# A fused recurrence and gated block on one core: 60 gate units in 56 slots instead of 60, and 25 instead of 24 output products in a slot

## The chip, the cores and the metric

The kernel runs on one core of one Trainium2 chip. The metric is the device time of one execution in microseconds (us). All engines of the core take part: PE (TensorE, the matmuls), DVE (VectorE), ACT (ScalarE), POOL (GpSimd) and SP (SyncE, which here issues every DMA of the stage that is described below).

## What is computed

The input is a sequence of 2048 tokens with 1024 features. After a layernorm two branches run, and the result is `x + s * silu(ffn)`:

```python
xn = _layernorm(x)
# recurrent branch
proj = xn @ W_in.T;  x, gate = proj[..., :2048], proj[..., 2048:]
x = silu(causal_conv4(x));  ts, B, C = rms(split(x @ W_x.T));  dt = softplus(ts @ W_dt.T + b_dt)
state = state * exp(dt * A) + (dt * x) * B          # per token, 2048 channels x 16 states
y = (state . C + x * D) * silu(gate);  s = y @ W_out.T
# gated block with 4-bit weights and low-rank parts
g = _qlinear(xn, gate_q, ...);  u = _qlinear(xn, up_q, ...);  f = _qlinear(silu(g) * u, down_q, ...)
out = x + s * silu(f)
```

A product of 32-bit numbers is made of 16-bit ones: each operand is split into a high and a low part, and three products (high with high, high with low, low with high) are added up in PSUM.

## The kernel before

**Two parts.** A first part (lines 180 to 1000) normalizes and transposes x, forms the convolved branch, dt, B and C, and stores what the second part reads. The second part is a loop over 256 **slots** that every engine goes through in its own queue. A slot is one state index n of one step; a step (16 slots) is 512 tokens of 512 channels. All engines hold the loop over slots as straight code and meet by semaphores alone.

**The scan, in every slot.** POOL multiplies the injection (L1660, one operation of 128x2048) some three slots ahead, in a ring of four. ACT forms four decays (L1384). DVE runs four scans (L1524), and between them it adds three transposed blocks of the slot before into the sum over states (`add_up`, L1542, and L1536 where n is 0); ACT and POOL handle the fourth block (L1422, L1672). PE transposes the slot before in four groups of four (`turn`, L1710). Before the first group of a slot PE waits for the four scans of the slot before; DVE's first `add_up` of a slot waits for that first group. In slots with n = 3, 7, 11, 15, from step 1 on, PE transposes one block back (`y_back`, L1721) and DVE makes one more operation (`d_u`, L1551).

**The other work, as filler of PE between the groups of transposes** (the function `piece` and its neighbours), by slot number s:

- s = 0 to 59, the **gate units**: unit u = s + 4 (u = 0 to 3 are made before the loop) is a tile of 128 gate channels for 512 tokens, 24 products, in four pieces of six (`gate_product`, L1733). In slot s + 1 ACT takes the tanh (L1442), DVE multiplies (L1576) into `gout[u % 2]`, and SP stores that to `gs_s` (L1250). DVE's multiplication of unit u waits until the store of unit u - 2 has landed, since both use one of two buffers. The weights come in halves of 128x512 f32: SP loads half h to `gr` (L1150), ACT scales and rounds it (L1403, L1406), POOL forms the low part (L1638).
- s = 60 to 147, the 88 FFN units, two products of eight double parts each (L1752, L1754, L1763).
- s = 150 to 213, the down product, four slots to each of 16 token tiles (L1780).
- s = 216 to 255, the **output product** with W_out: 1536 products in 32 results of 48, of which 24 are made in a slot (`out_product`, L1828). A result is added up by DVE (L1558) and POOL and stored by SP. The first 36 products read a quarter of W_out's converted halves, which SP loads after the last down product (L1339).
- After slot 255, the rest of the output products: 4 times (12 products and a `y_back`), then up to result 24, then a wait for the last step's y (`e_y`, loads; `e_lo`, four small operations of DVE and ACT that follow the last `y_back`, L1628), then the results 24 to 31.

**SP's queue.** SP goes through the same slots as a list of waits and DMA issues, in this order within a slot: W_out piece; in odd slots the broadcast load of B (`load_bb`, L1146), which waits for the injection of slot s + 2 to be done; the load of a gate half; the store of the gate unit made on PE in slot s - 2; conversions of the down weights (L1254, L1258); loads and stores of the FFN; where n is 2 the four loads of the next step (L1302, L1305, 512 KB each); y stores; down and output transfers. What waits in this list holds everything behind it.

**Order of the phases.** `FF0` is the slot in which the FFN begins, and `DOWN0`, `OUT0` follow from it; `DQ_AT` and `WO_AT` are the slots of the two weight conversions. The lines that set the amounts:

```python
FF0 = GATES - EARLY                       # 64 - 4 = 60
if s < FF0: gate_product(s + EARLY, 2 * u, 2 * u + 2)          # piece u of a slot, eighths of a unit
def out_cut(s): return 24 * (s - OUT0), 24 * (s - OUT0 + 1)
first = 24 * (SLOTS - OUT0)               # output products made before the loop ends
```

Of the kernel before, what the change touches and what calls it, by code (L numbers as in the profile page):

```python
# [33 lines left out]
T = 512  # L34
# [3 lines left out]
HK = H // P  # L38
DT = DI // P
J = 4  # L40
G = DT // J
IT = -(-I // P)
# [5 lines left out]
LEAD = 1  # L48
# [4 lines left out]
    "s_const s_gsc s_dec s_dub s_inj s_scan s_carry s_turn s_sum s_ev s_acc s_yt s_yev s_gate s_yhi s_parts s_ug0 s_ug1 "  # L53
    "s_ys0 s_ys1 s_u15 s_bb0 s_bb1 s_bb2 s_bb3 s_dt0 s_dt1 s_du0 s_du1 s_wq0 s_wq1 s_bt0 s_bt1 s_conv s_g s_u s_scg "
    "s_scu s_lg s_lu s_ex s_sg s_h s_hi s_lo s_hs0 s_hs1 z_in z_sc z_hi z_lo z_mm z_ex z_g z_st0 z_st1 c_in q_cv c_st "
# [5 lines left out]
SLOTS = STEPS * N  # L61
GATES = DT * C
EARLY = C
FF0 = GATES - EARLY
# [13 lines left out]
DQ_AT = tuple(7 * i // 3 for i in range(IT))  # L78
# [3 lines left out]
def mixer_kernel(nc, x, win, convw, convb, wx, wdt, bdt, alog, dskip, wout, gu_q, g_scale, u_scale,  # L82
# [3 lines left out]
    with whole:  # L86
# [85 lines left out]
        s_dec, s_inj = sem("s_dec"), sem("s_inj")  # L172
        z_in, z_sc, z_hi, z_lo, z_mm, z_ex, z_g = (sem("z_" + a) for a in "in sc hi lo mm ex g".split())
        inj = sb(whole, "inj", [P, RING, J, T])
        with ExitStack() as st:
# [52 lines left out]
            (f_const, f_nv, f_sd, f_xn, f_tp, f_xh, f_xl, f_sc, f_hi, f_lo, f_z, f_mm, f_cv, f_e, f_u, f_wx,  # L228
             f_hl, f_hs, f_sm, f_rv, f_rq, f_rm, f_tt, f_ts, f_tl, f_bt, f_pre, f_mx, f_nab, f_ex, f_ln, f_dt, f_a, f_b, f_ap,
             f_bl, f_bs, f_du, f_ru, f_dv) = (sem("f_" + a) for a in (  # L230
                "const nv sd xn tp xh xl sc hi lo z mm cv e u wx hl hs sm rv rq rm tt ts tl bt pre mx nab ex ln dt a b ap "
# [46 lines left out]
            with nc.Block() as block:  # L278
                @block.sync
                def _(sp):  # L280
# [78 lines left out]
                    for u in range(LAST + 2):  # L359
# [10 lines left out]
                        if u == LAST:  # L370
                            sp.wait_ge(f_mm, LEAD + LAST - 1)
                            for half in range(2):
                                sp.dma_start(gout[:, half, :], win[DT, :, half * T:(half + 1) * T]).then_inc(z_in, 16)
# [43 lines left out]
                    sp.dma_start(gr[:, :], win[DT + 1, :, 0:T]).then_inc(z_in, 16)  # L417
                    store_bt(C - 1)
                    sp.wait_ge(f_rm, LEAD + 4 * C)
                    sp.dma_start(gr_next[:, :], win[DT + 1, :, T:2 * T]).then_inc(z_in, 16)  # L420
# [16 lines left out]
                def _(act):  # L437
# [67 lines left out]
                    def gate_high(half, src):  # L505
                        act.activation(src, src, ACT.Copy, scale=WS).then_inc(z_sc, 1)
# [60 lines left out]
                    act.wait_ge(z_in, LEAD + 32)  # L567
# [21 lines left out]
                    act.wait_ge(z_in, LEAD + 64)  # L589
# [414 lines left out]
        with ExitStack() as st:  # L1004
# [48 lines left out]
            (s_const, s_gsc, s_dub, s_scan, s_carry, s_turn, s_sum, s_ev, s_acc, s_yt, s_yev, s_gate, s_yhi, s_parts,  # L1053
             s_u15, s_conv, s_g, s_u, s_scg, s_scu, s_lg, s_lu, s_ex, s_sg, s_h, s_hi, s_lo) = (sem("s_" + a) for a in (
                "const gsc dub scan carry turn sum ev acc yt yev gate yhi parts u15 conv g u scg scu lg lu ex sg h hi lo"
# [46 lines left out]

            def out_cut(s):

                return 24 * (s - OUT0), 24 * (s - OUT0 + 1)
# [33 lines left out]
            with nc.Block() as block:  # L1139
                @block.sync  # L1140
                def _(sp):
# [7 lines left out]
                    def load_gate(half, dst):  # L1149
                        sp.dma_start(dst, win[DT + half // 2, :, half % 2 * T:(half % 2 + 1) * T]).then_inc(z_in, 16)  # L1150
# [75 lines left out]
                    for m, src in enumerate((g_scale, u_scale)):  # L1226
                        sp.dma_start(gsc[:, m, :], src).then_inc(s_const, 16)
                    for s in range(SLOTS):
# [147 lines left out]
                def _(act):  # L1376
# [23 lines left out]
                    def gate_high(half, src):  # L1400
                        w, r = divmod(half, 2)
                        act.wait_ge(z_in, LEAD + max(16 * half + 16, 32))
# [26 lines left out]
                    act.wait_ge(s_const, LEAD + 32)  # L1429
# [4 lines left out]
                    for s in range(SLOTS):  # L1434
# [3 lines left out]
                        u = s - 1 + EARLY  # L1438
                        if EARLY - 1 <= u < GATES:
# [26 lines left out]
                        half = (s + EARLY + 3) // 2  # L1466
                        if s % 2 == 1 and half < 2 * DT:
                            gate_high(half, gr[:, :])
# [498 lines left out]
```

## Time and profile before

| what | us |
|---|---|
| median of 3 runs (lowest, highest) | 2778.59 (2778.08, 2783.23) |
| the profiled execution | 2781.2 |
| its span, first to last instruction | 2779.4 |
| gate units from slot 3 to the end of slot 59 | 424.45 |
| FFN, slots 60 to 147 | 815.75 |
| down product and its surroundings, slots 148 to 215 | 538.38 |
| output product, slots 216 to 255 | 289.20 |
| after the last slot | 133.67 |

The slot limits are read from the timeline of DVE: a slot begins with the first of its four scans. The page says that PE is busy for 97% of the span, DVE for 86%, POOL for 71% and ACT for 57%, with a mean granted TensorE clock of 0.993. The busy time of PE counts the modelled end of each matmul, so neighbours overlap in it; distances between starts tell what a piece takes. In a timeline row the first number is the start, the second the length, and a bracket names the idle time before it and what ended it. In a row of a stretch the numbers are the length, then the busy time of each engine with its instructions, the granted clock, the DMA engines' busy share and the rate in GB/s. A row of DMA issues ends with the size and the median time from issue to landing.

### The profile page before, as it was taken

Reading aid. Unit: us, or ns where it says so; the run is one execution under the profiler, and the core shown is the slowest. Engines: PE = TensorE matmul, PEld = TensorE weight load, DVE = VectorE, ACT = ScalarE, POOL = GpSimd, SP = SyncE. Lnnn points to the kernel's source line nnn. Section 1 sums busy time; section 2 is a strip of 40 time slices with the busy share of each in tenths; the row PEclk is TensorE's granted clock in tenths of the full one; section 3 lists DMA queues with packets and bytes.
Section 4 is the critical chain, followed back from the end, with each engine's and each line's share of the span. In section 5 each row is a group of like instructions: output and inputs, shape, how many; then the busy total and the mean of one; then the engine's idle time right before and its main releaser. Section 6 shows DMA issues by size and latency. Waiting matters only on the chain.

```text
span 2779.4 us, 42529 instructions
## 1 busy us (share of the span) xinstructions
PE 2691.1 (97%) x15444; PEld 1561.5 (56%) x15444; DVE 2402.2 (86%) x2916; ACT 1586.0 (57%) x2643; POOL 1985.6 (71%) x943
## 2 busy tenths in 40 slices
PE   6999999899999999999999999989999998999999
PEld 3545555455555555555555555556666665555644
DVE  5978877699999998888888888899999999999920
ACT  4444644666666667777777777654555455545500
POOL 2311223188999998889898989887889788999911
PEclk9999999999999999999999999999999999999999
DMA  7755476255455545454544454664554547666541
GB/s 241 236 174 192 134 276 197 99 159 177 158 189 177 162 126 169 129 161 121 168 132 146 129 166 122 206 179 137 137 149 120 157 124 228 179 182 189 147 131 57
DMA packets 338944, 448.79 MB, mean 161 GB/s; under 512 B 170640, under 2 KB 181136, under 8 KB 334704
## 3 DMA queue, kind: packets, MB, share of 16 engines
q1 hardware_dynamic: 338736, 446.08, 52.9%
q8 instruction: 123, 2.02, 0.3%
q14 instruction: 85, 0.70, 0.1%
HBM read 312.06 MB, written 133.94 MB: 160 GB/s over the span
## 4 chain that ended last, share of the span: by engine, by line
PE 52%; DVE 15%; issue 6%; POOL 3%; DMA 2%; ACT 1%; SPq 0%; DVEq 0%; POOLq 0%; ACTq 0%
PE xtp_turned L1710 11%; DVE inj L1524 8%; PE main_bank L1780 7%; PE main_bank L1752 7%; PE main_bank L1754 7%; DVE ysum L1542 5%; PE main_bank L1828 4%; PE misc_bank L1754 3%; PE misc_bank L1752 3%; PE misc_bank L1780 3%; PE misc_back L1794 2%; PE misc_bank L1828 2%; POOL inj L1660 2%; DMA h_s<-work 1%; DVE work L1576 1%
## 5 line engine op out<-in xcount | busy, mean ns | idle before, releaser
L1660 POOL TENSOR_TENSOR inj<-dd,bb 128x2048 f32<-128x2048 f32 x255 | 1156.4, 4535 | 246.5 <-PE xtp_turned L1710 245.6
L1710 PE MATMUL xtp_turned<-ident,inj 128*128 128x128 f32 x4096 | 626.9, 276 | 39.6 <-DVE inj L1524 25.7
L1524 DVE TENSOR_TENSOR_SCAN inj<-ssm_decay,carry,inj 128x512 f32<-128x512 f32 x512 | 650.6, 1271 | 3.0 <-ACT ssm_decay L1384 3.0
L1524 DVE TENSOR_TENSOR_SCAN inj<-main_decay,carry,inj 128x512 f32<-128x512 f32 x512 | 647.5, 1265 | 1.0 <-ACT main_decay L1384 0.9
L1710 PEld LDWEIGHTS xtp_turned<-ident,inj 128*128 128x128 f32 x4096 | 503.6, 142 | 253.1 <-DVE inj L1524 77.6
L1542 DVE SCALAR_TENSOR_TENSOR ysum<-xtp_turned,cT,ysum 128x512 f32<-128x512 f32 x721 | 526.9, 731 | 111.5 <-PE xtp_turned L1710 110.3
L1384 ACT ACTIVATE main_decay<-dd,aneg 128x512 f32<-128x512 f32 x511 | 351.3, 687 | 380.7 <-DVE inj L1524 380.2
L1384 ACT ACTIVATE ssm_decay<-dd,aneg 128x512 f32<-128x512 f32 x511 | 352.5, 690 | 313.0 <-DVE inj L1524 311.1
L1752 PE MATMUL main_bank<-xx,work 128*128 128x512 f16 x936 | 355.5, 380 | 1.0 <-ACT work L1397 1.0
L1754 PE MATMUL main_bank<-xx,work 128*128 128x512 f16 x936 | 355.5, 380 | 0.0
L1672 POOL TENSOR_TENSOR ysum<-ysum,work 128x512 f32<-128x512 f32 x239 | 306.5, 1282 | 10.5 <-ACT work L1422 10.5
L1733 PE MATMUL main_bank<-xx,work 128*128 128x512 f16 x960 | 234.5, 381 | 3.1 <-PEq L278 3.1
L901 PE MATMUL main_bank<-xx,work 128*128 128x512 f16 x1008 | 227.3, 383 | 4.0 <-DMA work<-w_s 3.4
L1422 ACT ACTIVATE work<-xtp_turned,cT 128x512 f32<-128x512 f32 x239 | 162.1, 678 | 45.3 <-PE xtp_turned L1710 30.3
L1828 PE MATMUL main_bank<-xx,work 128*128 128x512 f16 x768 | 185.2, 381 | 0.0
L1752 PE MATMUL misc_bank<-xx,work 128*128 128x512 f16 x472 | 178.9, 379 | 0.0
L1754 PE MATMUL misc_bank<-xx,work 128*128 128x512 f16 x472 | 178.9, 379 | 0.0
L901 PEld LDWEIGHTS main_bank<-xx,work 128*128 128x128 f16 x1008 | 97.7, 99 | 120.9 <-issue 9.0
L828 POOL TENSOR_TENSOR taps<-halo,inj 128x12 f32<-128x12 f32 x36 | 11.0, 334 | 199.4 <-DVE halo L636 199.4
L1733 PEld LDWEIGHTS main_bank<-xx,work 128*128 128x128 f16 x960 | 94.3, 98 | 82.8 <-issue 5.8
L1754 PEld LDWEIGHTS main_bank<-xx,work 128*128 128x128 f16 x936 | 91.7, 98 | 85.8 <-issue 0.5
L1752 PEld LDWEIGHTS main_bank<-xx,work 128*128 128x128 f16 x936 | 91.7, 98 | 84.2 <-ACT work L1397 1.2
(208 smaller groups left out, 4016.8 us busy)
## 6 DMA issues: line engine op xcount, KB each, us to landing
bb<-bt_s SPq DMA_DIRECT2D x128, 512.0 KB, 5.7
work<-w_s SPq DMA_DIRECT2D x48, 512.0 KB, 3.9
work<-in_gu_q SPq DMA_DIRECT2D x88, 256.0 KB, 3.4
h_s<-work SPq DMA_DIRECT2D x88, 256.0 KB, 3.9
u_s<-inj SPq DMA_DIRECT2D x64, 256.0 KB, 4.4
dd<-dt_s SPq DMA_DIRECT2D x32, 512.0 KB, 8.6
gs_s<-work SPq DMA_DIRECT2D x64, 256.0 KB, 6.0
us<-u_s SPq DMA_DIRECT2D x60, 256.0 KB, 5.2
```

Source lines behind the costliest of these rows:

```text
L901: mm = pe.matmul(main[u % 3][:, :], ww[:, u % 3, part, k * P:(k + 1) * P], xx[:, c, side, k, :], start=(k == 0 and part + side == 0), stop ...
L1384: act.activation(decay[j % 2][:, :], dtb[:, step % 2, j, :], ACT.Exp, scale=aneg[:, step % G * J + j, n:n + 1]).then_inc(s_dec, 1)
L1524: v.tensor_tensor_scan(inj[:, s % RING, j, :], decay[j % 2][:, :], inj[:, s % RING, j, :], carry[:, step % G * J + j, n:n + 1], ALU.mult, ...
L1542: v.scalar_tensor_tensor(dst, turned[t % 2][:, :], weight, dst, ALU.mult, ALU.add).then_inc(s_sum, 1)
L1660: pool.tensor_tensor(inj[:, e % RING, :, :], dub[:, step % 2, :, :], bb[:, e % 8:e % 8 + 1, :].broadcast_to([P, J, T]), ALU.mult).then_inc ...
L1672: pool.tensor_tensor(ysum[:, step % 2, ADDS, :], ysum[:, step % 2, ADDS, :], ev[:, :], ALU.add).then_inc(s_acc, 1)
L1710: mm = pe.transpose(turned[t % 2][:, j * P:(j + 1) * P], inj[:, s % RING, j, t * P:(t + 1) * P], ident[:, :])
L1733: mm = pe.matmul(bank[u % 3][:, :], gw[w % 2][:, part, h * P:(h + 1) * P], xx[:, c, side, h, :], start=(h == 0 and part + side == 0), stop ...
L1752: pe.matmul(dst[:, :], w, xx[:, p, 0, h, :], start=(h == 0), stop=False, skip_group_check=True)
L1754: mm = pe.matmul(dst[:, :], w, xx[:, p, 1, h, :], start=False, stop=False, skip_group_check=True)
L1780: mm = pe.matmul(bank[y % 3][:, :], hc[tile % 2][:, i, part, :], dw[:, i, half * T:(half + 1) * T], start=(r == 0), stop=False, skip_group ...
L1828: mm = pe.matmul(bank[z % 3][:, :], y, (wo_hi, wo_hi, wo_lo)[w][:, i, half * T:(half + 1) * T], start=(i == 0 and w == 0), stop=(i == DT - ...
```

## The change

`FF0` becomes 56, so every later phase begins four slots earlier (FFN at 56, down at 146, output at 212). The 60 units of the loop are 480 eighths, of which slot s makes those from 480 s / 56 to 480 (s + 1) / 56, that is 8 or 9, so 24 or 27 products; a unit no longer ends with a slot. ACT, DVE and SP take the units that were finished in the slot before (or two before, for SP) from the list `gates_done`, which has one unit for most slots and two for four of them, s = 13, 27, 41 and 55. The halves of the gate weights go in turn through `gr` and `gr_next`, with a semaphore to each, and are loaded when the half two before has been converted; the slots of the conversions are thinned out to the new pace (`GATE_HALF_AT`). The loads of two small scales count on a semaphore that was there already. In the output phase 25 products are made in a slot, so 1100 in 44 slots instead of 960 in 40, and 436 instead of 576 are left after the last slot; the four times 12 after it then end at product 1148, where result 24 begins at 1152. The conversions of the down weights and of W_out are moved with the phases.

```diff
-FF0 = GATES - EARLY
+FF0 = GATES - 2 * EARLY
...
-DQ_AT = tuple(7 * i // 3 for i in range(IT))
+DQ_AT = tuple(9 * i // 4 for i in range(IT))
+GATE_HALF_AT = {max(1, (2 * h - 7) * FF0 // (GATES - EARLY)): h for h in range(EARLY, 2 * DT)}
+OUT_MS = 25
...
+            def gate_cut(s):
+
+                return tuple((GATES - EARLY) * HK * r // FF0 for r in (s, s + 1))
+
+            def gates_done(s):
+
+                if not 0 <= s < FF0:
+                    return (EARLY - 1,) if s == -1 else ()
+                a, b = gate_cut(s)
+                return tuple(EARLY + m // HK for m in range(a, b) if m % HK == HK - 1)
+
             def out_cut(s):
 
-                return 24 * (s - OUT0), 24 * (s - OUT0 + 1)
+                return OUT_MS * (s - OUT0), OUT_MS * (s - OUT0 + 1)
...
-                    def load_gate(half, dst):
-                        sp.dma_start(dst, win[DT + half // 2, :, half % 2 * T:(half % 2 + 1) * T]).then_inc(z_in, 16)
+                    def load_gate(half):
+                        sp.wait_ge(z_lo, LEAD + half - 1)
+                        sp.dma_start((gr, gr_next)[half % 2][:, :], win[DT + half // 2, :, half % 2 * T:(half % 2 + 1) * T]
+                                     ).then_inc(z_in[half % 2], 16)
...
-                        half = (s + EARLY) // 2 + 2
-                        if s % 2 == 0 and half < 2 * DT:
-                            sp.wait_ge(z_lo, LEAD + half)
-                            load_gate(half, gr[:, :])
-                        u = s - 2 + EARLY
-                        if EARLY - 1 <= u < GATES:
+                        if s == 0:
+                            load_gate(EARLY)
+                        if s + 1 in GATE_HALF_AT:
+                            half = GATE_HALF_AT[s + 1]
+                            if half > EARLY:
+                                load_gate(half)
+                        for u in gates_done(s - 2):
                             w, c = divmod(u, C)
                             sp.wait_ge(z_g, LEAD + u + 1)
                             sp.dma_start(gs_s[w // J, c, :, w % J, :], gout[:, u % 2, :]).then_inc(z_st[u % 2], 16)
...
-                        u = s - 1 + EARLY
-                        if EARLY - 1 <= u < GATES:
+                        for u in gates_done(s - 1):
                             act.wait_ge(z_mm, LEAD + u + 1)
                             atleast(act, z_g, u)
...
-                        u = s - 1 + EARLY
-                        if EARLY - 1 <= u < GATES:
+                        for u in gates_done(s - 1):
                             v.wait_ge(z_ex, LEAD + u + 1)
                             atleast(v, z_st[u % 2], u // 2 * 16)
...
-                            cuts = tuple(out_cut(s)[0] + 6 * u for u in range(5))
+                            cuts = tuple(out_cut(s)[0] + OUT_MS * u // 4 for u in range(5))
...
                             if s < FF0:
-                                gate_product(s + EARLY, 2 * u, 2 * u + 2)
+                                a, b = gate_cut(s)
+                                for m in range(a + (b - a) * u // 4, a + (b - a) * (u + 1) // 4):
+                                    gate_product(EARLY + m // HK, m % HK, m % HK + 1)
...
-                    first = 24 * (SLOTS - OUT0)
+                    first = OUT_MS * (SLOTS - OUT0)
```

## Rows read from the trace of the kernel before

**Rows 1.** Stretches: gate slots 3 to 59, output slots 216 to 255, after the last slot.

```profile
577.95:1002.40 424.45, 410.10 (x2328) 242.01 (x2329) 422.35 (x468) 285.50 (x489) 382.12 (x163) 1.00 0.52 166
...
2356.53:2645.73 289.20, 285.25 (x1638) 171.69 (x1637) 285.80 (x310) 143.45 (x250) 268.11 (x121) 1.00 0.62 181
2645.73:2779.40 133.67, 128.65 (x610) 59.96 (x608) 19.96 (x30) 3.15 (x5) 21.18 (x17) 1.00 0.27 85
```

**Rows 2.** Stretches of four steady slots: gate (44 to 47), output (248 to 251).

```profile
882.79:912.54 29.75, 28.80 (x167) 17.06 (x165) 29.75 (x35) 20.60 (x36) 27.55 (x13) 1.00 0.58 165
...
2588.62:2617.18 28.56, 28.46 (x165) 17.17 (x164) 28.56 (x33) 14.56 (x26) 27.73 (x13) 1.00 0.47 126
```

**Rows 3.** Timeline of DVE, the first half of gate slot 45.

```profile
890.08 1.25 DVE L1524 TENSOR_TENSOR_SCAN inj<-main_decay,carry,inj 128x512 f32<-128x512 f32 x1
891.25 0.71 DVE L1542 SCALAR_TENSOR_TENSOR ysum<-xtp_turned,cT,ysum 128x512 f32<-128x512 f32 x1
891.90 1.26 DVE L1524 TENSOR_TENSOR_SCAN inj<-ssm_decay,carry,inj 128x512 f32<-128x512 f32 x1
893.09 0.65 DVE L1576 SCALAR_TENSOR_TENSOR work<-work,main_bank 128x512 f32<-128x512 f32 x1
893.66 0.73 DVE L1542 SCALAR_TENSOR_TENSOR ysum<-xtp_turned,cT,ysum 128x512 f32<-128x512 f32 x1
```

**Rows 4.** Timeline of PE in the same slot: transposes, a piece of six, transposes.

```profile
891.99 0.60 PE L1710 MATMUL xtp_turned<-ident,inj 128*128 128x128 f32 x4
892.43 1.46 PE L1733 MATMUL main_bank<-xx,work 128*128 128x512 f16 x6
893.72 0.60 PE L1710 MATMUL xtp_turned<-ident,inj 128*128 128x128 f32 x4
```

**Rows 5.** Timeline of PE and DVE in FFN slot 66, which began at 1055.14.

```profile
1056.88 0.60 PE L1710 MATMUL xtp_turned<-ident,inj 128*128 128x128 f32 x4
...
1057.52 0.75 DVE L1542 SCALAR_TENSOR_TENSOR ysum<-xtp_turned,cT,ysum 128x512 f32<-128x512 f32 x1 [1.12 <-PE xtp_turned L1710]
```

**Rows 6.** One line by itself, L1442: count, then ns least, median and most.

```profile
L1442 ACT ACTIVATE work<-main_bank x41: 571/578/583, 556.0 to 1004.3; 128x512 f32<-128x512 f32 x41
```

**Rows 7.** Timeline: a gate store's release (slots 42, 43), and DVE in slot 16.

```profile
873.66 4.53 POOL L1660 TENSOR_TENSOR inj<-dd,bb 128x2048 f32<-128x2048 f32 x1 [1.37 <-PE xtp_turned L1710]
...
878.22 0.37 SPq L1146 DMA_DIRECT2D bb<-bt_s  x1
...
878.63 0.47 SPq L1250 DMA_DIRECT2D gs_s<-work  x1
...
677.53 0.69 DVE L1576 SCALAR_TENSOR_TENSOR work<-work,main_bank 128x512 f32<-128x512 f32 x1 [0.79 <-DMA gs_s<-work]
```

**Rows 8.** DMA issues: all gate stores of slots 3 to 59, one of slot 15, a store after slot 255.

```profile
gs_s<-work SPq DMA_DIRECT2D x58, 256.0 KB, 6.0
...
gs_s<-work SPq DMA_DIRECT2D x1, 256.0 KB, 7.3
...
y_s<-us SPq DMA_DIRECT2D x1, 256.0 KB, 2.1
```

**Rows 9.** Timeline of PE in FFN slot 132.

```profile
1672.63 0.38 PE L1763 MATMUL main_bank<-xa,work 96*128 96x512 f16 x1 [2.12 <-ACT main_bank L1452]
```

**Rows 10.** The stretch around that wait.

```profile
1670.00:1678.00 8.00, 5.88 (x25) 2.98 (x24) 6.03 (x7) 6.70 (x12) 4.61 (x4) 0.79 0.22 70
```

**Rows 11.** Timeline of PE and DVE after the last slot.

```profile
2660.23 0.60 PE L1721 MATMUL misc_back<-ident,ysum 128*128 128x128 f32 x4
...
2663.11 0.69 DVE L1628 TENSOR_TENSOR dd<-dd 128x512 f16<-128x512 f32 x1
```

**Rows 12.** DMA issues: the first two loads of W_out, issued from 2340.41 on.

```profile
xx<-wo_s SPq DMA_DIRECT2D x2, 1024.0 KB, 9.1
```

**Rows 13.** Timeline of SP: the four loads of a step, slots 209 and 210.

```profile
2306.38 0.89 SPq L1302 DMA_DIRECT2D dd<-u_s  x2
2307.31 2.31 SPq L1305 DMA_DIRECT2D dd<-dt_s  x2
```

More of the change, by code:

```diff
@@ L171, in mixer_kernel @@
         z_st = [sem(f"z_st{b}") for b in range(2)]
-        s_dec, s_inj = sem("s_dec"), sem("s_inj")
-        z_in, z_sc, z_hi, z_lo, z_mm, z_ex, z_g = (sem("z_" + a) for a in "in sc hi lo mm ex g".split())
+        s_dec, s_inj, f_const = sem("s_dec"), sem("s_inj"), sem("f_const")
+        z_in = [sem(f"z_in{b}") for b in range(2)]
+        z_sc, z_hi, z_lo, z_mm, z_ex, z_g = (sem("z_" + a) for a in "sc hi lo mm ex g".split())
         inj = sb(whole, "inj", [P, RING, J, T])
@@ L372, in _ @@
                             for half in range(2):
-                                sp.dma_start(gout[:, half, :], win[DT, :, half * T:(half + 1) * T]).then_inc(z_in, 16)
+                                sp.dma_start(gout[:, half, :], win[DT, :, half * T:(half + 1) * T]).then_inc(z_in[half], 16)
                         if u >= 2:
@@ L505, in gate_high @@
                     def gate_high(half, src):
+                        act.wait_ge(z_in[half % 2], LEAD + 16 * (half // 2 + 1))
                         act.activation(src, src, ACT.Copy, scale=WS).then_inc(z_sc, 1)
@@ L566, in _ @@
                             low_high(LOW_AT[u - 1])
-                    act.wait_ge(z_in, LEAD + 32)
                     gate_high(0, gout[:, 0, :])
@@ L1051, in y_part @@
                 return us_of(step, j).bitcast(F16)[:, part * T:(part + 1) * T]
-            (s_const, s_gsc, s_dub, s_scan, s_carry, s_turn, s_sum, s_ev, s_acc, s_yt, s_yev, s_gate, s_yhi, s_parts,
+            (s_gsc, s_dub, s_scan, s_carry, s_turn, s_sum, s_ev, s_acc, s_yt, s_yev, s_gate, s_yhi, s_parts,
              s_u15, s_conv, s_g, s_u, s_scg, s_scu, s_lg, s_lu, s_ex, s_sg, s_h, s_hi, s_lo) = (sem("s_" + a) for a in (
-                "const gsc dub scan carry turn sum ev acc yt yev gate yhi parts u15 conv g u scg scu lg lu ex sg h hi lo"
+                "gsc dub scan carry turn sum ev acc yt yev gate yhi parts u15 conv g u scg scu lg lu ex sg h hi lo"
              ).split())
@@ L1401, in gate_high @@
                         w, r = divmod(half, 2)
-                        act.wait_ge(z_in, LEAD + max(16 * half + 16, 32))
+                        act.wait_ge(z_in[r], LEAD + 16 * w + 16)
                         act.activation(src, src, ACT.Copy, scale=WS).then_inc(z_sc, 1)
@@ L1465, in _ @@
                             act.activation(woh[:, :], wor[:, :], ACT.Copy).then_inc(w_hi, 1)
-                        half = (s + EARLY + 3) // 2
-                        if s % 2 == 1 and half < 2 * DT:
-                            gate_high(half, gr[:, :])
+                        if s in GATE_HALF_AT:
+                            half = GATE_HALF_AT[s]
+                            gate_high(half, (gr, gr_next)[half % 2][:, :])
                         exp(s, 3)
@@ L1641, in _ @@
                     for e in range(SLOTS + 6):
-                        half, odd = divmod(e + EARLY, 2)
-                        if odd == 0 and EARLY <= half < 2 * DT:
-                            gate_low(half, gr[:, :])
+                        if e - 3 in GATE_HALF_AT:
+                            half = GATE_HALF_AT[e - 3]
+                            gate_low(half, (gr, gr_next)[half % 2][:, :])
                         if e - 4 in WO_AT:
```

18 lines of the change are left out of this document (9 added, 9 removed).

## The prediction

> **What bounds the kernel now.** I read the stretches first, since the page's means (PE 97%, DVE 86%) lump stages with different limits. In the gate slots 3 to 59 DVE is busy for 422.35 of 424.45 us, and in output slots DVE (285.80) and PE (285.25 of 289.20) stand level [rows 1]. Four steady slots show it sharper: 29.75 us in the gate stage and 28.56 in the output stage, with DVE never idle in either [rows 2]. DVE's timeline then says what its slot is made of. Start to start, a scan and what follows it take 1.17 to 1.19, an addition 0.65 and the gate multiplication 0.57 [rows 3]. So a gate slot is 4 x 1.19 + 3 x 0.65 + 0.57 = 7.28 us, and one slot in four has a `d_u` of 0.64 more: 4 x 7.28 + 0.64 = 29.76, as measured.
>
> PE's rows of the same slot give its own need: a group of transposes takes 0.44, a piece of six products 1.29, hence 0.215 a product [rows 4]. Its gate slot is 4 x (0.44 + 1.29) = 6.92, below 7.28, and it waits for the scans at each slot's start. In FFN slots it is the other way round: DVE waits 1.12 for the first transposes [rows 5], so there PE sets the pace. I count 2779.4 of span; the profiled execution is 2.6 above the median, and the differences below are put on the median.
>
> **The gate stage.** DVE runs 53 slots from 3 on instead of 57. Its steady slot stays 7.28: the slots of 27 products need 6.92 + 3 x 0.215 = 7.57 on PE, but 24 of the 56 slots have 24, so the mean is 25.7 products, 7.29 with nothing else. DVE's first addition needs PE's first transposes, which take 0.64 from PE's start to DVE's; DVE comes to it 1.17 after its slot begins. PE may thus run up to 0.53 late at no cost, and it starts 0.1 late when it is ahead. Followed slot by slot, the lag eats through that cushion now and then, 1.2 us in all.
>
> Four slots (14, 28, 42, 56) now carry two gate multiplications. `ex` is one buffer, so the second tanh waits for the first multiplication, and the second multiplication for that tanh of 0.58 [rows 6]. Each of these slots is 0.65 + 0.58 + about 0.1 = 1.34 longer. The first three lie in this stage. It also has one `d_u` fewer. So 53 x 7.28 + 10 x 0.64 + 3 x 1.34 + 1.2, and the 2.45 of irregular slots that 424.45 has beyond 57 x 7.28 + 11 x 0.64, make 399.9: **-24.5**.
>
> **A new wait.** The multiplication of unit u + 2 needs the store of unit u landed. Before, each unit had a slot of its own, two slots from u to u + 2. After a double slot f (14, 28, 42) units u and u + 1 are multiplied in f and u + 2 already in f + 1. The store of u is issued in SP's slot f + 1, and f + 1 is odd, so it stands behind `load_bb`, which waits for POOL's injection for a later slot. In the trace that injection ends at 873.66 + 4.53 = 878.19, the `load_bb` follows at 878.22 and the store at 878.63, all inside slot 43 [rows 7]; from where slots begin this is 3.3 to 3.75 us in. After a double slot, longer by 1.34 and with POOL therefore further ahead, I take 2.9. DVE would come to its multiplication 3.0 into its slot. The landing takes 6.0 in the median of 58 stores, 7.3 in one, 2.1 for a store that is alone [rows 8]. I take 6.0, as its circumstances are these; the bounds are 2.1 and 7.3. That leaves 2.9 + 6.0 - 3.0 = 5.9 us of wait on DVE, three times: **+17.7** (6.0 to 21.6). That this wait can bind is seen once before, 0.79 in slot 16 [rows 7]. Behind DVE's multiplication stand two scans and two additions, and for these PE waits, with ACT and POOL a little later. POOL, three slots ahead, and SP's other entries are not pressed. The wait after slot 56 does not occur, since unit 63 is the last.
>
> PE's own wait behind these comes to a few us each, and its clock may fall behind them. A wait of 2.12 in the FFN shows it [rows 9]: over the eight us around it the granted clock is a mean of 0.79 [rows 10], full clock (2.4 GHz) with a part at half (1.2 GHz), which is (1 - 0.79) x 8 = 1.7 us of work. Since DVE, not PE, sets the pace here, most of that is absorbed: I take 0.6 each, 1.8 in all (0 to 5.1). PE then enters the FFN 0.6 after DVE rather than 0.3 ahead: +0.9. Slot 1's SP order costs about 0.5. Gate stage: -24.5 + 17.7 + 1.8 + 0.9 + 0.5 = **-3.6**.
>
> On the store's landing a page speaks against the wait. By the Trainium skill, "DMA: Bandwidth & Descriptors", section "Anatomy of one DMA — SWDGE (gpsimd) path", a DMA issued by GpSimd takes about 2.0 us and its bytes over 436 GB/s; as an estimate that is 2.6 us for 256 KB, and would leave 2.5 us of wait each and a sum some 10 us lower. The row of 58 stores at 6.0 disagrees with it, these come from SP and share the engines with other traffic, and only the store that is alone, at 2.1, comes near.
>
> **The output stage.** PE makes 25 products a slot: four slots need 4 x (4 x 0.44 + 25 x 0.215) + 0.44 for `y_back` = 29.0, more than DVE's 28.56. PE becomes the bound by a little. 44 slots are 11 x 29.0 = 319.0; with 3.6 that the 40 slots of before have beyond 10 x 28.56, and 0.6 until PE's lag has built up, 323.2. Against 289.20: **+34.0**. Output and tail together are no gain: what the tail loses the loop takes on, in slots that have no spare room.
>
> **The tail.** 576 - 436 = 140 products leave it: 140 x 0.2155 = -30.2. But the last wait now has less cover. Before, 96 products lay between the fourth 12 (with its `y_back`) and result 24; now 4 do. The last `y_back` starts at 2660.23 and takes PE to 2660.67; the last operation for `e_lo` ends on DVE at 2663.11 + 0.69 = 2663.80 [rows 11]. Four products reach 2661.5, so PE waits 2.3, and its clock may fall behind that as in rows 10: I take 0.8, between 0 and 1.7. Tail: -30.2 + 2.3 + 0.8 = **-27.1**.
>
> **Costed at nothing.** The two weight buffers remove a wait that neither PE nor DVE has in steady slots, where DVE is full [rows 2]. The weight halves' conversions come at the new pace, and ACT and POOL have room in gate slots (285.50 and 382.12 of 424.45 [rows 1]); POOL at nine tenths is the cover that would go first. The moved conversions collide with the step loads in as many FFN slots as before (66 and 82 instead of 114 and 130); two waits like that of [rows 9] bound it, 4.2 either way. The FFN and down slots keep their work and merely start earlier.
>
> **Sum.** -3.6 + 34.0 - 27.1 = +3.3, so 2778.59 + 3.3 = **2782**. A difference of 0.2%, 5.6 us, is about what a measurement of this kernel can tell from no change: "same" is 2773.0 to 2784.2. With the bounds of the clock, of the store and of the conversions this case's own range is 2775 to 2790.
>
> **Rival 1, faster: the stores land at once.** If the three stores land like the one that is alone, the wait is 2.9 + 2.1 - 3.0 = 2.0 each, 11.7 less in all: 2770. With no wait at all, it is 2782 - 17.7 = 2764. For it: around the store only a `load_bb` and perhaps a gate half of 256 KB are in flight. Against: the median of 58 stores in the same surroundings.
>
> **Rival 2, slower: W_out comes late.** The first 36 output products read what SP loads after the last down product. Before, the two loads were issued from 2340.41 and landed in 9.1 [rows 12], by about 2351, against slot 216 at 2356.53: 5.5 us of slack. Now the output stage begins at slot 212, and the step loads of slot 210 (2 MB; SP takes 0.89 + 2.31 = 3.2 to issue them [rows 13]) stand directly before them in the queue, where four slots lay between. Two 1024 KB loads took 9.1, a small one alone 2.1, so 2 MB ahead cost about 7.0, with the issue at most 10.2; against 5.5 PE would be 1.5 to 4.7 late, and up to 1.7 more by the clock. PE being the bound there, nothing gives it back: +4.8, about 2787. It decides as soon as the step loads hold the transfers up by more than 5.5. Against it: the wait for these loads' own buffers may release them early.
>
> A third way, a gate stage bound by PE, I leave out: 53 slots at a mean of 7.29 with ten `y_back`s are 391, under the 399.9 that DVE needs.
>
> **Chances.** Forecast 0.57 (0.40 same, 0.17 slower), rival 1 0.25 (0.22 faster, 0.03 same), rival 2 0.18 (slower). The range 2766 to 2790 leaves out the end of rival 1 without any wait and the double mishaps.
>
> **What would show it.** Slots 15, 29 and 43 of about 13 us, with DVE's multiplication idle for about 5.9 behind the DMA of `gs_s`; slots 14, 28, 42 at 8.6 and the others at 7.28; 29.0 for four output slots, with DVE now waiting for PE; PE idle for about 2.3 before its last 384 products. A first output piece that waits for the DMA of `xx` would be rival 2; waits for `gs_s` of 2 us or less rival 1. It is wrong altogether if steady gate slots lengthen, or if POOL's injections come late.

## The result, and the profile after

| what | before | after |
|---|---|---|
| median of 4 runs (lowest, highest), us | 2778.81 (2778.08, 2783.23) | 2801.49 (2799.13, 2805.04) |
| the profiled execution | 2781.2 | 2800.0 |
| its span | 2779.4 | 2798.2 |

The changed kernel is slower: the ratio of the times is 1.0078, with a 95% interval from 1.0066 to 1.0091. The forecast was 2782, with a range from 2766 to 2790. The two profiled executions lie 18.8 us apart, the medians 22.7; what follows accounts for the 18.8.

The first view is that of stretches of the changed kernel: gate slots 3 to 55, FFN slots 56 to 143, output slots 212 to 255, after the last slot, slot 15, and four steady output slots. The columns are those of [rows 1].

```profile
578.96:1009.54 430.58, 405.08 (x2253) 238.04 (x2252) 396.32 (x438) 270.54 (x461) 353.70 (x150) 0.98 0.49 157
1009.54:1829.20 819.66, 810.45 (x4484) 466.48 (x4483) 717.69 (x815) 586.42 (x1049) 711.61 (x356) 1.00 0.48 145
2368.28:2690.80 322.52, 320.75 (x1847) 194.56 (x1846) 316.71 (x342) 157.88 (x275) 299.49 (x136) 1.00 0.63 180
2690.80:2798.20 107.40, 100.22 (x470) 46.62 (x468) 17.90 (x27) 3.15 (x5) 17.06 (x14) 0.98 0.25 88
672.38:685.75 13.37, 8.30 (x39) 4.70 (x40) 7.39 (x10) 5.06 (x9) 6.45 (x4) 0.84 0.50 178
2632.78:2661.79 29.01, 29.01 (x170) 17.71 (x169) 28.77 (x32) 14.57 (x26) 27.85 (x13) 1.00 0.46 118
```

Set against the same stretches of before, the account is:

| stretch | before | after | difference | forecast |
|---|---|---|---|---|
| up to slot 3 | 577.95 | 578.96 | +1.0 | +0.5 |
| gate units | 424.45 | 430.58 | +6.1 | -4.1 |
| FFN | 815.75 | 819.66 | +3.9 | 0 |
| down product and around | 538.38 | 539.08 | +0.7 | 0 |
| output slots | 289.20 | 322.52 | +33.3 | +34.0 |
| after the last slot | 133.67 | 107.40 | -26.3 | -27.1 |
| sum | | | +18.7 | +3.3 |

(The forecast's gate stage was -3.6 with 0.5 for slot 1, which stands in the first line here.) The output share came out as forecast, the gate stage and the FFN did not. DVE, which was busy for 422.35 of 424.45 us in the gate stage before, is now busy for 396.32 of 430.58. Its waits in that stretch, by what it waited for (us in total, times, the longest):

```profile
DVE work L1591 <- DMA gs_s<-work: 29.1, 14, 7.1
DVE ysum L1558 <- PE xtp_turned L1725: 4.1, 3, 1.7
```

Before, the first of these was 1.5 us in 3 waits, and the second did not occur:

```profile
DVE work L1576 <- DMA gs_s<-work: 1.5, 3, 0.8
```

The timeline of DVE shows the first double slot (14), the slot after it, and the slot after that:

```profile
668.09 0.69 DVE L1591 SCALAR_TENSOR_TENSOR work<-work,main_bank 128x512 f32<-128x512 f32 x1 [2.38 <-DMA gs_s<-work]
...
681.46 0.69 DVE L1591 SCALAR_TENSOR_TENSOR work<-work,main_bank 128x512 f32<-128x512 f32 x1 [5.98 <-DMA gs_s<-work]
...
688.62 0.75 DVE L1558 SCALAR_TENSOR_TENSOR ysum<-xtp_turned,cT,ysum 128x512 f32<-128x512 f32 x1 [1.61 <-PE xtp_turned L1725]
```

The middle row is the wait that the prediction describes, in slot 15, which began at 672.38. SP issued the two stores of the double slot there, behind `load_bb`, and they landed 6.0 us later (SP's timeline, then the DMA issues of these two):

```profile
674.78 0.38 SPq L1160 DMA_DIRECT2D bb<-bt_s  x1
675.20 1.15 SPq L1267 DMA_DIRECT2D gs_s<-work  x2
```

```profile
gs_s<-work SPq DMA_DIRECT2D x2, 256.0 KB, 6.0
```

675.20 is 2.8 us into the slot; the prediction took 2.9 and 6.0. The waits in slots 15, 29 and 43 are 5.98, 7.14 and 5.96, together 19.1 against a forecast of 17.7. The other eleven, 10.0 us in all, were not forecast: 4.6 of them lie in the double slots 14, 28 and 42, and 5.4 in even slots of which the slot before has its store late (6, 10, 18, 32, 34, 36, 38, 46). Slot 33 shows how that comes about. It began at 825.89; the rows are of POOL, SP and DVE.

```profile
823.91 1.17 POOL L1653 TENSOR_TENSOR work<-work 128x512 f16<-128x512 f32 x1
825.03 4.54 POOL L1675 TENSOR_TENSOR inj<-dd,bb 128x2048 f32<-128x2048 f32 x1
...
829.59 0.37 SPq L1160 DMA_DIRECT2D bb<-bt_s  x1
830.01 0.47 SPq L1165 DMA_DIRECT2D work<-in_win  x1
830.52 0.43 SPq L1267 DMA_DIRECT2D gs_s<-work  x1
...
836.79 0.69 DVE L1591 SCALAR_TENSOR_TENSOR work<-work,main_bank 128x512 f32<-128x512 f32 x1 [0.54 <-DMA gs_s<-work]
```

The store is issued at 4.63 into the slot. Before, in the same slot, it was at 3.23 (804.05, the slot having begun at 800.82), and in slot 43 at 3.76 [rows 7]. Two things stand ahead of it now. The load of a gate half has its place between `load_bb` and the store and takes half a microsecond to issue; and POOL's conversion of a half ends just when the injection that `load_bb` waits for begins, so this injection ends later, and `load_bb` goes out at 3.70 into the slot instead of 2.82. Both were in the other slots before: halves were loaded in even slots of SP and converted ahead of even injections, while `load_bb` is in odd slots. With 56 slots the halves come every 1.87 slots, and in two stretches (slots 2 to 14 and 28 to 42) they fall on the wrong parity. Slots 18 and 46 (1.3 us) lie outside these stretches; `load_bb` is late in 17 and 45 too, at 3.7, with no half and no conversion ahead of it, and why stays open.

In the FFN, PE's timeline has three waits where there were two, of which [rows 9] is one:

```profile
1126.83 0.38 PE L1778 MATMUL main_bank<-xa,work 96*128 96x512 f16 x1 [1.84 <-ACT main_bank L1468]
...
1276.09 0.38 PE L1778 MATMUL misc_bank<-xa,work 96*128 96x512 f16 x1 [1.64 <-ACT misc_bank L1468]
...
1425.76 0.38 PE L1778 MATMUL main_bank<-xa,work 96*128 96x512 f16 x1 [2.04 <-ACT main_bank L1468]
```

They lie in slots 68, 84 and 100. ACT is late there because the store of `h_s` that frees its buffer, issued in the slot before (67), landed only 7.8 us after its issue (first row), against 3.6 in slot 65 (second):

```profile
h_s<-work SPq DMA_DIRECT2D x1, 256.0 KB, 7.8
...
h_s<-work SPq DMA_DIRECT2D x1, 256.0 KB, 3.6
```

One more wait of PE, for a converted weight in slot 137, is 1.85 us; in the slot of the same work before it was 0.98.

After the last slot PE waits 2.21 us before its last 384 products, as forecast (2.3):

```profile
2708.92 3.48 PE L1843 MATMUL main_bank<-xx,bb 128*128 128x512 f16 x8 [2.21 <-issue]
```

### The profile page after: what moved, and what is told of

It is laid out like the page before. It is cut to its first block, busy times and chain, and to the rows that moved or that the text cites. A ratio compares the mean times of both kernels' runs of the same rounds, so it can differ in the third digit from the quotient of the medians.

```text
span 2798.2 us, 42531 instructions
## 1 busy us (share of the span) xinstructions
PE 2693.4 (96%) x15444; PEld 1567.5 (56%) x15444; DVE 2410.1 (86%) x2916; ACT 1587.3 (57%) x2643; POOL 1987.2 (71%) x943
## 4 chain that ended last, share of the span: by engine, by line
PE 60%; DVE 7%; POOL 4%; DMA 4%; issue 4%; ACT 1%; SPq 0%; DVEq 0%; POOLq 0%; ACTq 0%
PE xtp_turned L1725 13%; PE main_bank L1795 7%; PE main_bank L1843 7%; PE main_bank L1767 7%; PE main_bank L1769 7%; DVE inj L1540 4%; PE misc_bank L1769 3%; PE misc_bank L1767 3%; POOL inj L1675 3%; PE misc_bank L1795 3%; PE misc_bank L1843 3%; DMA gs_s<-work 3%; DVE ysum L1558 2%; PE misc_back L1809 2%; PE main_bank L1748 2%
```

## The experiments

Each kernel was timed in five rounds against the kernel before, on the same chip in each group. Ratios are to the kernel before, with 95% intervals; the changed kernel's is 1.0078 [1.0066, 1.0091]. Waits are those of gate slots 3 to 55.

**The place of the stores in SP's list.** First the store goes ahead of the half, but stays behind `load_bb`:

```diff
+                        for u in gates_done(s - 2):
+                            ...
                         if s == 0:
                             load_gate(EARLY)
                         if s + 1 in GATE_HALF_AT:
                             ...
-                        for u in gates_done(s - 2):
-                            ...
```

> The changed kernel with one move in SP's list: the store of a finished gate unit stands ahead of the load of a gate half, still behind the load of B. Theory (the store's place in SP's list): the shorter waits of DVE for gs_s, some 10 us in all, come from stores that are issued at 4.3 to 4.8 us into an odd slot, behind the half, instead of 3.2 to 3.8; with the order turned they are issued there again, these waits fall to 1 to 3 us in all, and the three waits after the double slots stay at about 6 each. Time about 2792, 7 to 11 less than the changed kernel. Rival (traffic): what is late is the landing, since the half and the load of B share the DMA engines with the store; then landings stay at 6 to 7 and the waits shrink by half a microsecond each at most, about 3 us in all, 2798.

Measured: 2792.09, ratio 1.0038 [1.0026, 1.0050]. DVE's waits in the gate stage of its profiled execution:

```profile
DVE work L1591 <- DMA gs_s<-work: 25.9, 13, 6.3
DVE ysum L1558 <- PE xtp_turned L1725: 3.1, 3, 1.7
```

The median is the theory's, the waits are not: 17.9 are in slots 15, 29 and 43, so the shorter ones are still 8.0 where 1 to 3 were expected. The stage is 5.4 shorter, 425.2; the profiled execution, 2795.68, is the slowest of the five. So the half's place in the list is one part of it and not the whole: in slots 31, 33, 37 and 41 the store is still issued at 4.2 to 4.5, since `load_bb` itself is late.

Then the store goes ahead of `load_bb` too, to the top of SP's slot:

```diff
+                        for u in gates_done(s - 2):
+                            ...
                         if s % 2 == 1 or s == 0:
                             ...
                                 load_bb(pair)
```

> The changed kernel with the store of a finished gate unit first in SP's slot, ahead of the load of B and so of its wait for POOL's injection, and ahead of the half. Theory: all waits of DVE for gs_s go (29.1 us in slots 3 to 55 and 1.6 in slot 56), and with them PE's late restarts (4.1): about 34 us less, 2767, under the kernel before. The four double slots stay 1.3 longer than the others. Rival (the landing itself is what takes the time after a double slot): a store that is issued some 4 us earlier still lands 6 us later, so the waits after double slots fall from 6 to about 2 and the sum from 2801 to about 2778.

Measured: 2767.80, ratio 0.9950 [0.9937, 0.9963]. The stretches are its gate slots 3 to 55 and slot 15, the waits those of the gate stage:

```profile
576.56:976.13 399.57, 393.99 (x2251) 235.02 (x2252) 394.60 (x438) 270.54 (x461) 354.90 (x150) 1.00 0.54 173
...
667.27:674.54 7.27, 7.13 (x41) 4.34 (x42) 7.27 (x9) 5.06 (x9) 5.97 (x4) 1.00 0.26 82
```

```profile
DVE work L1591 <- DMA gs_s<-work: 3.9, 3, 1.7
```

The gate stage takes 399.6, where the prediction's sum without any wait was 399.9. Slot 15 falls from 13.37 to 7.27. What is left are 3.9 in the double slots. So all of the loss in this stage is the wait for the stores and what follows it, and the DMA traffic does not force it: nearly the same bytes are moved in less time (173 against 157 GB/s). The rival, a wait bounded by the landing, fell for two reasons. The first store of a pair now goes out in the double slot itself, 3.7 us into slot 14, which is 9.65 long; that is 8.8 us earlier than in the changed kernel and not 4, enough even for a landing of 6 us. And it does not take 6 us: the two stores of slot 14, ahead of `load_bb`, land in 2.6 (first row), the next one, in slot 15 behind `load_bb` and a load of down weights, in 7.8 (second).

```profile
gs_s<-work SPq DMA_DIRECT2D x2, 256.0 KB, 2.6
...
gs_s<-work SPq DMA_DIRECT2D x1, 256.0 KB, 7.8
```

To separate the three long waits from the shorter ones, only the stores of the double slots were put first:

```diff
+                        for u in gates_done(s - 2) if len(gates_done(s - 2)) == 2 else ():
+                            ...
                         if s % 2 == 1 or s == 0:
...
-                        for u in gates_done(s - 2):
+                        for u in gates_done(s - 2) if len(gates_done(s - 2)) == 1 else ():
```

> The changed kernel with the stores of the two units of a double slot first in SP's slot (slots 15, 29, 43, 57), all other stores where they were. Theory: the three waits after the double slots (5.98, 7.14, 5.96) go and with them PE's late restarts (4.1), so 23 less than the changed kernel, about 2778; the shorter waits before even slots, 10 us, stay. Rival (one cause for all waits, the traffic on the DMA engines): the long waits shrink by little, 2795.

Measured: 2777.43, ratio 0.9994 [0.9986, 1.0003]; the gate stage takes 408.1, 22.5 less than in the changed kernel.

```profile
DVE work L1595 <- DMA gs_s<-work: 10.0, 8, 2.5
DVE ysum L1562 <- PE xtp_turned L1729: 1.3, 2, 0.9
```

The shorter waits stay at 10.0, the long ones are gone. With this one edit the changed kernel is level with the kernel before, which is where the prediction had put it with the long waits in.

**What makes the shorter waits.** Two more kernels took one of the two suspects each. The first is `store_before_half` with POOL's conversion moved behind the injection:

```diff
-                        if e - 3 in GATE_HALF_AT:
-                            ...
                         if (0 < e < SLOTS):
                             ...
+                        if e - 3 in GATE_HALF_AT:
+                            ...
```

> The kernel of store_before_half, in which POOL also forms the low part of a gate half after the injection of its slot instead of ahead of it. Theory: where the halves are converted in even slots (2 to 14, 28 to 42), POOL's conversion stands directly ahead of the injection that the load of B waits for, so SP issues the load of B and the store behind it at 4.2 to 4.5 us into the slot; behind the injection it no longer does: the stores of these slots are issued at 3.3 to 3.8, as in the kernel before, the shorter waits fall from 8 to under 3, and the time is about 5 less than store_before_half, 2787. Rival: the conversion is not what makes the injection late, the stores are issued as before and the time stays at 2792; or POOL's later low part holds up PE, and it rises.

Measured: 2788.95, ratio 1.0031 [1.0018, 1.0043], and 22.5 us of waits for `gs_s`, 6.2 of them short where under 3 were expected. In slots 32 to 40 no wait is left (two in store_before_half, 1.1 us), and the stores of slots 31 to 41 are issued at 3.5 to 4.1. But waits of 0.6 to 1.7 remain in slots 6, 18, 22 and 46, and the interval overlaps with that of store_before_half: in time this run doesn't decide.

The second is the changed kernel with the halves loaded in even slots only:

```diff
-                        if s + 1 in GATE_HALF_AT:
-                            half = GATE_HALF_AT[s + 1]
+                        for at in (s, s + 1) if s % 2 == 0 else ():
+                            half = GATE_HALF_AT.get(at, EARLY)
```

> The changed kernel with every load of a gate half in an even slot of SP, as in the kernel before; stores and loads of B where they were. Theory: in the stretches where the halves are loaded in odd slots (1 to 13, 27 to 41) the load puts off the store behind it by its own issue of half a microsecond and lengthens the landing by sharing the DMA engines; in even slots it does neither, so the shorter waits fall from 10 us to about 4 (what POOL's later injection leaves), the three after the double slots stay: 2795. Rival: the halves do nothing to the stores, no difference, 2801; or a half that is loaded later holds up ACT's conversion and PE, and the time rises.

Measured: 2798.99, ratio 1.0066 [1.0052, 1.0079], which overlaps with the changed kernel's.

```profile
DVE work L1591 <- DMA gs_s<-work: 27.7, 12, 6.9
DVE inj L1540 <- ACT ssm_decay L1401: 3.5, 3, 2.3
...
DVE inj L1540 <- ACT main_decay L1401: 1.4, 4, 0.3
```

The waits in slots 32 to 38, 2.1 in all, are gone, but the shorter ones are still 8.5, where 4 were expected, and new waits for ACT's decays stand in front of the scans (slots 11 to 13 and 32 to 35). That ACT gets its halves later explains these, but was not tested by itself. Theory and rival are both half right, and nothing is won: the stage takes 431.6.

**The output share.**

```diff
-OUT_MS = 25
+OUT_MS = 24
```

> The changed kernel with 24 instead of 25 output products in a slot, in its 44 slots. Theory (the prediction's terms for the output share): PE is no longer the bound in these slots, 11 x (29.0 - 28.56) = 4.8 us less there; 44 products more after the last slot, 9.5 us more; the wait of 2.2 before the last results goes, since 48 products cover it. About +2 us, 2803. Rival (25 in a slot is what makes the changed kernel slow): 10 us or more less.

Measured: 2802.71, ratio 1.0075 [1.0063, 1.0088]: no difference from the changed kernel that can be told, and far from the rival's 10. In its trace four output slots take 28.55 and the wait before the last results is gone, so the terms are as expected; they cancel (output slots and tail together take 432.0 instead of 429.9).

The kernel before with 25 in a slot, in the three places where it has 24 or 6:

```diff
-                return 24 * (s - OUT0), 24 * (s - OUT0 + 1)
+                return 25 * (s - OUT0), 25 * (s - OUT0 + 1)
-                            cuts = tuple(out_cut(s)[0] + 6 * u for u in range(5))
+                            cuts = tuple(out_cut(s)[0] + 25 * u // 4 for u in range(5))
-                    first = 24 * (SLOTS - OUT0)
+                    first = 25 * (SLOTS - OUT0)
```

> The kernel before with 25 output products in each of its 40 slots and nothing else changed. Theory: the output slots take 10 x (29.0 - 28.56) + 0.6 = 5.0 more, the tail 40 x 0.2155 = 8.6 less with its last wait still covered by 104 products: 3.6 less, 2775. Rival (each product moved into a slot costs as much there as it saves after the loop): no difference, 2779.

Measured: 2777.88 against 2781.27 in the same group, ratio 0.9984 [0.9976, 0.9993]: 3.4 us less, where 3.6 was expected. Four steady output slots of it:

```profile
2592.33:2621.33 29.00, 29.00 (x170) 17.71 (x169) 28.76 (x32) 14.55 (x26) 27.79 (x13) 1.00 0.45 119
```

**The FFN.** The changed kernel with W_out's conversions away from the step loads:

```diff
-WO_AT = tuple(FF0 + 11 * w // 4 for w in range(2 * DT))
+WO_AT = tuple(s for s in range(FF0, FF_END) if s % N > 4 and s % 2)[:2 * DT]
```

> The changed kernel with the conversions of W_out put into odd slots with n from 5 to 15, none near the step loads of n = 2. Theory: PE's waits in slots 68, 84 and 100 (1.84, 1.64, 2.04) come from stores of h_s that land 7.8 to 8.0 us after their issue, instead of 3.7, because the step loads and the stores and load of W_out's conversion are in flight with them; without that overlap slots 68, 84 and 100 take 8.9 instead of 10.6 to 11.0, and the time is 5 less, 2796. Rival: the step loads alone (2 MB) delay the stores, and the waits stay; then no change, or up to 4 more by the denser conversions.

Measured: 2794.01, ratio 1.0047 [1.0034, 1.0059]; the FFN takes 813.8 instead of 819.7, and slots 68, 84 and 100 take 9.06, 8.89 and 9.16. The store of `h_s` of slot 67 now lands in

```profile
h_s<-work SPq DMA_DIRECT2D x1, 256.0 KB, 6.1
```

so in this slot the step loads alone put it off by 2.5 us, which PE hardly feels, and the conversion's stores and load by the next 1.7, for which PE waits.

**A version that beats both.** `store_first`, W_out's conversions as above, and shorter pieces before the last wait:

```diff
-                        out_product(first + 12 * j, first + 12 * j + 12)
+                        out_product(first + 9 * j, first + 9 * j + 9)
                         y_back(STEPS - 1, j, back)
-                    first += 12 * J
+                    first += 9 * J
```

> The kernel of store_first with two more edits: W_out's conversions as in wout_away, and 4 times 9 instead of 12 output products between the last four transposes back. Theory: 16 products instead of 4 then cover the wait for the last low part, so PE's wait of 2.2 goes; with 5 from the conversions the time is 2767.8 - 7 = 2761, under both kernels. Rival: the last transposes back are then limited by DVE's operations between them, and the wait only moves: 2763.

Measured: 2756.06, ratio 0.9912 [0.9898, 0.9925]. PE's timeline before the last 384 products:

```profile
2664.68 0.60 PE L1736 MATMUL misc_back<-ident,ysum 128*128 128x128 f32 x4
2665.12 3.62 PE L1843 MATMUL misc_bank<-xx,work 128*128 128x512 f16 x16
2668.57 5.34 PE L1843 MATMUL main_bank<-xx,bb 128*128 128x512 f16 x24
```

Sixteen products cover the wait, and no idle time stands before the last ones. The time is 5 under what was expected: W_out's conversions had brought some 7.5 in wout_away where 5 was counted on, and output slots and tail together take 427.1 us instead of 429.8 in store_first.

Last, the kernel before with the edits that apply to it: its stores first, W_out's conversions away, 25 products.

> The kernel before (60 gate units in 60 slots) with the three edits that helped elsewhere: stores first in SP's slot, W_out's conversions away from the step loads, 25 output products in a slot. Theory: 3.4 from the output products, 1.5 from the waits for gs_s, 5 from the conversions: 10 less than the kernel before, about 2770. The changed kernel with the same edits and the shorter pieces before its last wait took 2756, so spreading the gate units over 56 slots would be worth 12 to 14 by itself (the prediction's sum without the wait for the stores gives 14). Rival: the edits bring as much to the kernel before as to the changed one, 2757, and the 56 slots are worth nothing.

Measured: 2768.45, ratio 0.9954 [0.9942, 0.9967]. So of the gain of the version above, 0.46% comes from edits that help the kernel before as well, and 0.42% (some 12 us; the two intervals lie 0.17% apart) remain for the 56 slots, once the long waits for their stores are gone; the shorter pieces, some 3 us, which only the changed kernel needs, are among them. By the stretches of the two profiled executions the gate stage is 21.8 us shorter than in the kernel before with its three edits (400.0 against 421.8), and 8.8 of that go back in the output slots and the tail, 2.4 in the FFN.

## Why the prediction was wrong

It forecast no change to be told, +3.3 us; the stretches of the profiled executions add up to +18.7, so it missed by 15.4, of which 10.2 are in the gate stage and 3.9 in the FFN. The steps that failed are two that it put at nothing, the new pace of the weight halves' conversions and the FFN, and with them its account of the double slot, in which it brought only one unit forward where two come early. The steps, in its order:

- **Gate stage without waits**: 399.9 forecast, 399.6 in store_first. Right, though not term by term: the 399.6 hold 3.9 of waits in the double slots, which took 9.65, 9.28 and 8.98 where 8.6 was forecast, and in these waits the second tanh (2.0 in the forecast) is hidden; of the lag of PE (1.2) little is seen.
- **The new wait**: right in place, cause and size, 19.1 against 17.7; 1.2 of the excess is slot 29, where a half's load too stood ahead of the store, which left at 4.50. store_first_doubles shows its worth: 22.5 us of the stage. The rival of stores that land at once did not occur: they took 5.6 to 6.2 in those slots.
- **The wait that it left out**: not only unit u + 2 comes a slot early, unit u + 1 does too. In slot 14 DVE is done with unit u 3.7 us into the slot; the store of u - 1, which it needs, was issued 6.78 into slot 13 and landed 6.55 later, 6.0 into slot 14. These waits are the 4.6 in slots 14, 28 and 42, of which the tanh would have taken about 2.0 anyway; 3.9 are still there in store_first.
- **"Costed at nothing": "The weight halves' conversions come at the new pace"**: the step that failed first. It asked whether ACT and POOL have time for the conversions, and they have. It didn't ask in which slot of SP's list their loads now fall, and ahead of which injection POOL's part stands. The store had little room for that: by the prediction's own numbers one that is issued at 3.8 and lands 6.0 later is there 2.5 into the slot after, and DVE comes to it at 3.0. The cost was 5.4 us in eight even slots, 4.2 of them in the two stretches of wrong parity. That the stores' lateness is the cause is shown by store_first, where none of the eight is left; how it divides between the half's issue, POOL's order and longer landings is not settled, since each edit by itself took away only some of them. The conversions of the down weights, whose slots moved as well, were not varied.
- **PE's clock behind the waits**: 0.6 each, 1.8 in all, against 4.1 of DVE waiting for PE in slots 16, 30 and 44. The granted clock over slot 15 was 0.84. It wasn't absorbed. In slot 15 PE had stood idle for 4.93 us and went on at half clock, with no lead over DVE left; that this is why DVE then waits is read from the timeline, not tested. PE's timeline at the end of slot 15 shows the half clock:

```profile
684.63 1.91 PE L1748 MATMUL misc_bank<-xx,work 128*128 128x512 f16 x4
686.33 1.49 PE L1748 MATMUL main_bank<-xx,work 128*128 128x512 f16 x3
```

  Four products take 686.33 - 684.63 = 1.70 from start to start, 0.425 each, where 0.215 is usual [rows 4]: that is 1.2 GHz instead of 2.4.
- **The sum of the stage**: waits for stores 29.1 - 17.7 = +11.4, waits for PE 4.1 - 1.8 = +2.3, what is left without both 430.6 - 29.1 - 4.1 = 397.4 against 399.9, -2.5 (the tanh and the lag, which the waits hide), and -0.9 for the late entry into the FFN, of which no run shows a term of its own. That is 10.3, and the stage is 10.2 over its forecast.
- **The FFN at nothing**: the second step that failed, +3.9, but not at the collisions. The prediction counted 66 and 82 against 114 and 130 and missed the step loads of slot 98, whose neighbours 97 and 100 carry a conversion; PE's timeline shows three waits where there were two. Yet these three cost no more than the two: slots 68, 84 and 100 are 1.9, 1.7 and 2.1 longer than slots of the same kind, 5.7 in all, and before it was 1.8 in slot 116 and 2.2 and 1.8 in slots 132 and 133, 5.7 as well, since the clock fell behind the wait in 132 (2.12 of wait, and (1 - 0.85) x 11.08 = 1.7 of clock) and stayed at 1.00 in all three. So this term came out near nothing by luck. The rows are slots 132 and 133 of before, then slots 100 and 56 of the changed kernel:

```profile
1665.78:1676.86 11.08, 8.96 (x42) 4.97 (x41) 8.11 (x11) 5.86 (x12) 7.40 (x5) 0.85 0.27 95
1676.86:1687.73 10.87, 10.87 (x59) 5.97 (x58) 7.97 (x10) 7.49 (x14) 9.70 (x5) 1.00 0.62 189
...
1418.99:1429.98 10.99, 8.95 (x50) 5.04 (x49) 8.10 (x10) 5.61 (x11) 7.82 (x5) 1.00 0.46 159
...
1009.54:1019.16 9.62, 8.42 (x48) 4.69 (x47) 8.06 (x10) 4.96 (x10) 9.27 (x5) 1.00 0.49 169
```

  What the FFN lost is elsewhere. The double slot 56, to which the prediction gave no term, took 9.62 against 7.29 for the FFN's first slot before, +2.3, with 1.56 of wait for a store in it; with that store in the same place it was 8.8 in the profiled executions of out_24 and wout_away and 9.7 in that of halves_even. Slot 116, behind the step loads of 114, adds 0.5 and slot 137 0.9; why the latter grew was not tested. A part of the 3.9 is spread: the FFN of before_out_25, which is that of the kernel before, took 817.9 and not 815.8. wout_away takes back 5.9, more than the change had added, as the kernel before had such waits too.
- **Output and tail**: right, +33.3 and -26.3 against +34.0 and -27.1; 29.01 for four slots, the wait 2.21. The clock behind that wait cost more than the 0.8 that was taken: 0.79 over eight us, (1 - 0.79) x 8 = 1.7, which is about the difference in the tail:

```profile
2708.00:2716.00 8.00, 7.08 (x26) 2.91 (x27) 1.92 (x4) 0.09 (x1) 2.48 (x2) 0.79 0.50 174
```

  out_24 and before_out_25 confirm the price of a product in a slot against one after it. **Rival 2** did not occur: W_out's second load landed 0.26 into slot 212, with PE not waiting for it.

## What to carry to other kernels

When a step changes its pace, look for the parity of everything it issues: a load or a conversion that moves by one slot can land ahead of a store that has half a microsecond of room. Put a store that frees a buffer ahead of waits that have nothing to do with it in the same queue; here that one move was worth some 34 us and turned a loss into a gain. And count collisions by listing the slots with their neighbours on both sides, not by one offset that was seen to hurt, and then price each: three cost here what two had cost before, and step loads with the same neighbours as those of slot 98, at 114, cost only 0.5.

## What was not expected of the hardware

A store of 256 KB takes about 6 us to land where it follows the 512 KB load of B in SP's queue (5.3 to 8.8 in the gate stage of the changed kernel, where all but three do), but 2.4 to 2.8 when it is issued late in slots 15, 29 and 43 with little else under way. The estimate of 2.6 us that follows from the fit in the Trainium skill ("DMA: Bandwidth & Descriptors", section "Anatomy of one DMA — SWDGE (gpsimd) path"), which is for DMAs issued by GpSimd, agrees with the second and not with the first.

store_first shows what makes the difference. In its slots 3 to 55 the 27 stores issued in odd slots, with `load_bb` in front of them, landed in 5.1 to 8.7 us, 6.7 in the median. Of the 29 issued in even slots, 26 landed in 2.4 to 5.7, 3.1 in the median; the other three, in slots 18, 34 and 50 behind the 2 MB of step loads, in 7.8 to 9.1. The clearest are those with one thing or nothing issued in the 6 us before them: five stores with `load_bb` alone in front (slots 19, 21, 23, 25, 43) took 5.1 to 6.5, six with nothing in front (slots 8, 12, 16, 20 and the second of 14 and of 28) 2.4 to 3.9. So a landing depends on what was issued just ahead of it, and moving a store ahead of a large load both sends it earlier and lets it land sooner. No run moved `load_bb` by itself, so this is a reading of the pattern in one trace.
